# Routed experts' second product: inner width cut 128 + 48 instead of 88 + 88, with the high and low parts of the 48 rows in one stationary tile, and the next pair's input transposed first

## What is computed

```python
scores = softmax(xt @ gate_w.T); top_w, top_idx = top_k(scores, 2)       # 8 experts, 2 per token
for e in range(8):
    h = silu(xt @ w1[e].T) * (xt @ w3[e].T)      # inner width 176
    y = y + dense_w[:, e:e + 1] * (h @ w2[e].T)  # 176 -> 256
z = silu(xt @ sw1.T) * (xt @ sw3.T) @ sw2.T      # shared expert, inner width 352
x = x + y + z
```

## Time and profile before

| | us |
|---|---|
| median of three runs | 510.48 |
| lowest and highest | 510.15, 511.11 |
| the profiled execution, its own time | 510.24 |
| its span, first to last instruction | 508.4 |
| TensorE busy | 456.6 (90%) |
| VectorE busy | 275.3 (54%) |
| ScalarE busy | 232.9 (46%) |
| GpSimd busy | 193.2 (38%) |

### The profile page before, as it was taken

The page is one execution under the profiler, slowest core; times in us unless marked ns, Lnnn a source line. Parts: engine busy times, 40 slices in busy tenths (PEclk is TensorE's granted clock), DMA queues, the critical chain, the costliest instruction groups (busy, mean ns, idle before and its releaser), DMA issues.

```text
span 508.4 us, 9181 instructions
## 1 busy us (share of the span) xinstructions
PE 456.6 (90%) x2849; PEld 379.9 (75%) x2850; DVE 275.3 (54%) x573; ACT 232.9 (46%) x467; POOL 193.2 (38%) x190
## 2 busy tenths in 40 slices
PE   0549979999999459999999999997899999999996
PEld 0348978888888349999999999996846765675663
DVE  0124347877667324444444444447486677677755
ACT  0313403444444314555555555543275577548655
POOL 5776000477777770000000000005764576567210
PEclk9868968999999959999999999999799999999999
DMA  3774884133333263545454445422321242223102
GB/s 81 237 233 142 322 296 137 44 144 140 140 144 134 101 229 91 153 145 148 139 149 142 148 136 150 141 93 81 105 84 62 64 123 84 84 84 108 60 8 76
DMA packets 44452, 65.90 MB, mean 130 GB/s; under 512 B 5437, under 2 KB 36925, under 8 KB 44211
## 3 DMA queue, kind: packets, MB, share of 16 engines
q1 hardware_dynamic: 36067, 44.00, 27.3%
q0 software_dynamic: 8096, 20.49, 12.9%
q10 hardware_dynamic: 264, 1.08, 0.6%
HBM read 32.00 MB, written 25.17 MB: 112 GB/s over the span
## 4 chain that ended last, share of the span: by engine, by line
PE 69%; POOL 15%; DMA 7%; issue 5%; DVE 2%; ACT 1%; DVEq 0%; ACTq 0%; SPq 0%; POOLq 0%
POOL slots_in L359 13%; PE bank L925 13%; PE bank L926 12%; PE bank L927 12%; PE bank L1185 12%; PE bank L1204 5%; PE bank L1065 3%; PE bank L1087 3%; DMA sw2st<-in_sw 3%; PE bank L966 3%; PE bank L944 2%; PE bank L1151 2%; PE bank L956 1%; POOL wrow L338 1%; DMA wrow<-in_table,rowi 1%
## 5 line engine op out<-in xcount | busy, mean ns | idle before, releaser
L373 POOL DMA_INDIRECT ga<-slots_out,slot x32 | 33.5, 1048 | 166.3 <-SPq L318 157.7
L359 POOL DMA_INDIRECT slots_in<-xt,slot x64 | 65.5, 1024 | 62.9 <-DVEq L718 43.7
L784 DVE TENSOR_TENSOR hrl<-bank,hrh 88x512 fp32r<-88x512 f32 x36 | 24.7, 687 | 69.6 <-ACT hrh L482 69.6
L1185 PE MATMUL bank<-h,wg 128*128 128x512 fp8e4 x256 | 61.6, 380 | 0.8 <-DVE h L848 0.8
L925 PE MATMUL bank<-w13h,xgl 128*128 x144 | 49.5, 343 | 0.0
L1185 PEld LDWEIGHTS bank<-h,wg 128*128 128x128 fp8e4 x256 | 22.2, 98 | 34.8 <-ACT ff L538 14.7
L927 PE MATMUL bank<-w13h,xgh 128*128 x144 | 46.4, 322 | 0.0
L926 PE MATMUL bank<-w13l,xgh 128*128 x144 | 46.3, 322 | 0.0
L944 PE MATMUL bank<-xres,bd 128*128 128x256 f32 (+1 forms) x64 | 21.5, 494 | 24.8 <-DVE bd L592 24.8
L536 ACT ACTIVATE gel<-bank 128x512 bf16<-128x512 f32 x64 | 40.5, 633 | 5.8 <-PE bank L1185 2.8
L488 ACT ACTIVATE yr<-bank 128x512 f32<-128x512 f32 x36 | 21.5, 597 | 44.3 <-PE bank L927 44.3
(11 more groups left out here) (160 smaller groups left out, 1120.1 us busy)
## 6 DMA issues: line engine op xcount, KB each, us to landing
xg<-slots_in SPq DMA_DIRECT2D x36, 256.0 KB, 2.8
slots_out<-yr SPq DMA_DIRECT2D x36, 256.0 KB, 2.2
xres<-in_x SPq DMA_DIRECT2D x8, 512.0 KB, 8.3
xt<-xtr SPq DMA_DIRECT2D x8, 512.0 KB, 3.9
xs<-xt SPq DMA_DIRECT2D x8, 512.0 KB, 3.3
out_x<-fin SPq DMA_DIRECT2D x7, 512.0 KB, 3.0
w13raw<-in_rw SPq DMA_DIRECT2D x1, 2816.0 KB
slots_in<-zero POOLq DMA_DIRECT2D x2, 1024.0 KB, 6.8
```

Of the source, the lines that this page charges most:

```text
L359: pool.indirect_dma_start(out=slots_in, out_offset=bass.IndirectOffsetOnAxis(slot[:, k, t:t + 1], 0), in_=xt[:, t, :], in_offset=None).the ...
L373: pool.indirect_dma_start(out=buf[:, g % 2, j, :], out_offset=None, in_=slots_out, in_offset=bass.IndirectOffsetOnAxis(slot[:, k, g * GT + ...
L1185: ins = pe.matmul(bank[bk][:, :], wg8[:, kk, half, c * P:(c + 1) * P], h8[:, k, kk, :], start=(kk == 0), stop=(kk == KC - 1))
```

## The change

The inner width of 176 is cut into 128 and 48. The 128 are treated as before, with three matmuls per tile. For the other 48, `routed_mul` writes the product twice into `hr`, at columns 128 and 192, with zeros between (the zeros are written once ahead of the loop); the transpose brings the two copies to rows 0 to 47 and 64 to 111 of one tile. `routed_h_lo` turns the second copy into its low part in place, by a second subtraction on 48 partitions. `w2` holds the 48 weight rows at both places too, with zeros between. One matmul 112 rows deep then gives high x high + low x high, and one 48 rows deep high x low. So a slot tile takes five matmuls and not six. The second weight array on the way from DRAM grows from 88 to 128 partitions of 16 KB (1408 to 2048 KB). In `routed`, `routed_T(n + 1)` moves ahead of `routed_hT(n - 1)`.

```diff
-        w2h = at("w2h", [HALF, E, 2 * D], F32R)
-        w2l = at("w2l", [HALF, E, 2 * D], F32R)
+        w2h = at("w2h", [P, E, 2 * D], F32R)
+        w2l = at("w2l", [P, E, 2 * D], F32R)
...
-        hr = at("hr", [P, 2, INNER], F32, pr)
-        hrh = at("hrh", [HALF, 4 * P], F32R, pr)
-        hrl = at("hrl", [HALF, 4 * P], F32R, pr)
+        hr = at("hr", [P, 2, 2 * P], F32, pr)
+        hrh = at("hrh", [P, 2, 2, P], F32R, pr)
+        hrl = at("hrl", [P, 2, P], F32R, pr)
...
-                act.activation(hrh[:, :], bank[4][0:HALF, :], ACT.Copy).then_inc(s("hr_hi"), 1)
+                act.activation(hrh[:, :, :, :].rearrange("p a b c -> p (a b c)"), bank[4][:, :], ACT.Copy).then_inc(s("hr_hi"), 1)
...
-                    dve.tensor_tensor(hr[:, j, :], silr[:, j, :], bank[j][:, INNER:2 * INNER],
+                    dve.tensor_tensor(hr[:, j, 0:P], silr[:, j, 0:P], bank[j][:, INNER:INNER + P], ALU.mult)
+                    dve.tensor_tensor(hr[:, j, P:2 * P].rearrange("p (a b) -> p a b", a=2)[:, :, 0:REST],
+                                      silr[:, j, P:INNER].unsqueeze(1).broadcast_to([P, 2, REST]),
+                                      bank[j][:, INNER + P:2 * INNER].unsqueeze(1).broadcast_to([P, 2, REST]),
                                       ALU.mult).then_inc(s("hr_ready"), 1)
...
-                dve.tensor_tensor(hrl[:, :], bank[4][0:HALF, :], hrh[:, :].bitcast(F32),
+                of_tile = bank[4][:, :].rearrange("p (a b c) -> p a b c", a=2, b=2)
+                dve.tensor_tensor(hrl[:, :, :], of_tile[:, :, 0, :], hrh[:, :, 0, :].bitcast(F32), ALU.subtract)
+                low = slice(LO_AT, LO_AT + REST)
+                dve.tensor_tensor(hrh[low, :, 1, :], of_tile[low, :, 1, :], hrh[low, :, 1, :].bitcast(F32),
                                   ALU.subtract).then_inc(s("hr_split"), 1)
...
-                        ins = pe.transpose(bank[4][0:HALF, col:col + P], hr[:, j, c * HALF:(c + 1) * HALF], ident)
+                        ins = pe.transpose(bank[4][:, col:col + P], hr[:, j, c * P:(c + 1) * P], ident)
...
-                    for c in range(2):
-                        h_at = slice((j * 2 + c) * P, (j * 2 + c + 1) * P)
-                        wh, wl = (w[:, bass.ds(experts[j], 1), c * D:(c + 1) * D].rearrange("p a f -> p (a f)")
-                                  for w in (w2h, w2l))
-                        ins = three(bank[5 + k][:, j * D:(j + 1) * D], hrh[:, h_at], hrl[:, h_at], wh, wl,
-                                    c == 0 and j == 0, c == 1)
+                    dst = bank[5 + k][:, j * D:(j + 1) * D]
+                    wh, wl = (w[:, bass.ds(experts[j], 1), 0:D].rearrange("p a f -> p (a f)") for w in (w2h, w2l))
+                    three(dst, hrh[:, j, 0, :], hrl[:, j, :], wh, wl, j == 0, False)
+                    both = w2h[0:LO_AT + REST, bass.ds(experts[j], 1), D:2 * D].rearrange("p a f -> p (a f)")
+                    rest = w2l[0:REST, bass.ds(experts[j], 1), D:2 * D].rearrange("p a f -> p (a f)")
+                    pe.matmul(dst, hrh[0:REST, j, 1, :], rest, start=False, stop=False, skip_group_check=True)
+                    ins = pe.matmul(dst, hrh[0:LO_AT + REST, j, 1, :], both, start=False, stop=True, skip_group_check=True)
...
+                routed_T(n + 1, k)
                 routed_hT(n - 1, n == 1 if first else False)
-                routed_T(n + 1, k)
                 routed_up(n, 1 - k, now)
```

More of the change, by code:

```diff
@@ L26 @@
 SHARED = 2 * INNER
-HALF = INNER // 2
+REST = INNER - P
+LO_AT = 64
 SC = 118
@@ L88, in adaln_ffn @@
         w13l = at("w13l", [P, E, KC * SHARED], F32R)
-        w2h = at("w2h", [HALF, E, 2 * D], F32R)
-        w2l = at("w2l", [HALF, E, 2 * D], F32R)
+        w2h = at("w2h", [P, E, 2 * D], F32R)
+        w2l = at("w2l", [P, E, 2 * D], F32R)
         after_routed = base[0]
         w13raw = at("w13raw", [P, E, KC * SHARED], F32, [after_routed - 8 * 2 * D * E - 4 * KC * SHARED * E])
-        w2raw = at("w2raw", [HALF, E, 2 * D], F32, [after_routed - 4 * 2 * D * E])
+        w2raw = at("w2raw", [P, E, 2 * D], F32, [after_routed - 4 * 2 * D * E])
         xt_at = base[0]
@@ L790, in _ @@
             add_shared(GROUPS - 2)
+            for j in range(2):
+                dve.tensor_copy(hr[:, j, P:2 * P].rearrange("p (a b) -> p a b", a=2)[:, :, REST:LO_AT],
+                                zero[:, 0:2 * (LO_AT - REST)].rearrange("p (a b) -> p a b", a=2))
             routed_mul(0)
@@ L1284 @@
     table = np.concatenate([L0_cond_weights.reshape(E * CH, CH), fside_8xS_0.reshape(E * CH, 1), np.zeros((E * CH, 1), f)], 1)
+    rw2 = np.zeros((P, E, 2, D), f)
+    rw2[:, :, 0] = L0_ffn_w2.transpose(2, 0, 1)[:P]
+    for at in (0, LO_AT):
+        rw2[at:at + REST, :, 1] = L0_ffn_w2.transpose(2, 0, 1)[P:]
     l1w = np.stack([L1_cond_W.T[:P], L1_cond_W.T[P:],
@@ L1297 @@
         "rw13": _by_partition(np.concatenate([L0_ffn_w1, L0_ffn_w3], 1).transpose(0, 2, 1)).reshape(P, E, -1),
-        "rw2": _by_partition(L0_ffn_w2.transpose(0, 2, 1), HALF).reshape(HALF, E, -1),
+        "rw2": rw2.reshape(P, E, -1),
         "l1w": l1w,
```

## The result

The changed kernel takes 531.4 us (530.93 to 531.85, four runs) against 510.76 (510.15 to 511.11) for the kernel before on the same chip: ratio 1.0405, 95% interval 1.0387 to 1.0423, 20.6 us slower. The forecast was 7.5 us faster.

What follows compares the result with a forecast made beforehand. It took TensorE's matmul time in the routed stage as the bound. Terms -8.6 - 0.3 + 0.1 + 1.3 = -7.5 us took the profiled 510.24 to 502.7, 503.0 as median; range 500.7 to 507.

Steps and rivals of the forecast that it cites:

- the term of the 48-row matmul: Second product: matmuls 48 or 112 rows deep were assumed to cost no more than those with 88, 0.119 us each.
- rival 3: Second product: each change of height drains the array, 0.16 us, four per pair, +23.0 us, 526.0 in all; chance 0.06.
- Two matmuls fewer per pair: Routed stage on TensorE: two matmuls fewer per tile pair, 36 x 2 x 0.119 us, saving 8.57 us.
- The order of the transposes: Routed loop: hr's transposes come 0.44 us later, the low part is usable at 253.96, still in time, so no stall.
- the slack of 0.05: Routed pair: low part usable 0.05 us before TensorE asks for its tile, in place of 0.41 before the change.
- rival 1: Routed pairs: low part 0.1 us later than worked out, TensorE stalls in 35 pairs, +4.7 us, 507.7; chance 0.11.
- The heads of the loop: Hardware-loop heads: TensorE's queue runs less far ahead, gaps grow by half of 0.36 us, 7 x 0.18 = +1.3 us.
- The bound of 0.36: Loop heads: the queue passes its low-part wait 0.36 us later, so each gap grows by 0 to 0.36 us.
- The weights' DMA: Second routed array, 640 KB larger, queued ahead of xs for the second group: landing not delayed, 0 us.
- rival 2: Weights' DMA: the added rows delay xs by 3.4 us, 506.4 in all; chance 0.05.
- The first and last pair: Ends of the routed stage: first pair gains 0.3 us in the wait for hr, last pair loses 0.1 on the low part.
- the clock: After the routed stage: earlier work may meet TensorE's clock fall or rise elsewhere, -1 to +1 us, 0 in the sum.

Runs made afterwards that it cites:

- halves_flat: Changed kernel with that matmul 112 rows deep, old transpose order, low-part wait split in two, TensorE's seven-round loop written out; 502.0 us, ratio 0.9816 to kernel before.
- reordered version: Changed kernel with the second product reordered: six matmuls of both tiles, two 48 rows deep, then two 112 rows deep; 520.33 us, ratio 1.0167 to kernel before.

## Why the prediction was wrong

**The step that failed** is the term of the 48-row matmul, put at nothing in the sentence "That 48 or 112 rows in place of 88 cost nothing more is an assumption". It took the steps of all matmuls to be alike and had no row with 64 rows or fewer. In its place the runs showed 0.39 us for each visit to such a matmul, 0.78 per pair, 28.1 in all, and nothing from 65 rows on. The price was named in rival 3 and given a chance of 0.06. Rival 3 was right in the place and in the count, four changes of height in a pair; its price of 0.16 us for each was low, they cost 0.195. With 0.78 for 0.64, rival 3 would have read 503.0 + 28.1 = 531.1; that this comes so near to 531.4 is partly luck, since smaller terms below were off too. Its argument against itself, that rows with 88 and 128 mix without a gap, was true and meant nothing: the limit is between 64 and 65. The rule cited there from the Trainium skill ("TensorEngine Tiling (Array Packing)", Tiling Modes), that a change of tiling mode drains TensorE, fits the late starts in the trace (steps of 0.21 in place of 0.12 into and out of the short matmuls), and the 64 of its Performance Considerations is where the runs put the limit. No record names a mode, and the kernel asked for no tiling, so that it is such a change of mode is not shown. A rule without a price and without a row deserved more than 0.06 when the change rests on the first instruction of that kind in the program.

**Two matmuls fewer per pair**, -8.57 us: right. With 65 or 112 rows the plain pair is 4.00 us, and 3.98 in the old order, which is 4.22 less two steps of 0.12.

**The order of the transposes.** The chain on ScalarE came out as worked out: from the first transposes to the high part 1.07 us (253.68 to 254.75; worked out 1.08), to the low part 1.70 (worked out 1.70). VectorE's two subtractions took 0.87 and not 0.75, since the second starts 0.44 after the first and not 0.33. So the low part was ready at 256.25, and TensorE's load of it started 0.13 later (256.38), as worked out. But that load would have gone at 256.31, with the matmul before it: the slack of 0.05 was in truth a lack of 0.07. The matmul still came in its usual step of 0.16 (256.31 to 256.47), which rival 1 had named as its own counter-argument. What I left out is that the queue needs the low part earlier than the array.

**The heads of the loop**, +1.3 with ends 0 and 2.5. Of the eight readings of the word the first and the last cost less than the six between. In the changed kernel the rounds together take 2.2 us more than as many plain pairs, against 1.4 before: a rise of 0.8, inside the range. That is luck. The slow short matmuls gave the queue time. Without them (112 rows) it is 8.4 us, 0.93 and 0.21 at each of the six heads between, a rise of 7.0. The bound of 0.36 counted only the later wait. It left out the round after the head, 0.2. It also left out that ten matmuls give the queue less to hide behind than twelve. So even with the height settled, the forecast of 503.0 would have been missed: the version with the matmul 112 rows deep and all else as in the change took 509.25.

**The weights' DMA** at 0: right; rival 2 did not happen.

**The first and last pair and the clock** cannot be told apart at their size: in the changed profile the granted clock rises some 2 us earlier at the start of the stage, which is more than the term. The first transposes of hr still wait, 0.46 us where it was 0.78, which is the 0.3 forecast. At the last pair TensorE waits 0.34 us for the low part where it was 0.15.

The sum of the result: pairs 36 x 0.56 = 20.2, heads +0.8, last pair +0.2, and -1.3 for the first round, which became 0.7 us shorter although its second product costs 0.56 more; together 19.9. From the stage's first transposes to the first gather the profiles show 20.1, the runs 20.6 for the whole.

**Other versions.** halves_flat beats both kernels: 9.4 us under the kernel before, about 30 under the changed one by their ratios (0.9816 against 1.0405). It keeps the change's idea (two matmuls fewer per pair) and undoes its order. The role of single parts of VectorE's chain was not tried, and why the round behind a head is 0.2 us longer in the new order is open.

## What to carry to other kernels

When a stream of full-height matmuls gets one of 64 rows or fewer (48 and 64 were measured), it pays for going there and coming back, about three matmuls' worth here; pad it past 64 rows, or put all such matmuls of a stage side by side. A wait that just fits on the array can still be late for the instruction queue, whose lead has to cover branches and register loads later on. So when work is taken out of a loop, look at the loop heads, and compare the distance between rounds, not the busy share.

## What was not expected of the hardware

- The limit in depth is sharp: 64 rows 0.38 us for the record and 532 us in all, 65 rows 0.28 and 511.
- Across the change of height no stationary tile is loaded ahead: load and matmul start at the same time (253.14 and 253.14, 253.45 and 253.45). Between two neighbours of one height the load is 0.1 us ahead again, also with 48 rows (253.61 and 253.73 in the reordered version).
- Two subtractions of 256 columns each start 0.44 us apart although each takes 0.42, while a subtraction of 512 columns lets the next instruction start 0.09 us before its end. Why the second does not overlap was not tried.
- The branch's lead over the last matmul and the step to the next transposes add up to 1.27 us in six kernels with leads from 0.22 to 0.93.
- Branch, counter and the reading of one word keep TensorE's queue for about 1.1 us; the reading alone (0.30 for the load, 0.16 and 0.02 behind it) was hidden whole once the branch was gone.
